# Values matmuls in two halves between the scores, and the last group's end work in small parts

## The chip, the cores and the metric

The kernel runs on one core of a Trainium2 chip. The metric is the device time of one execution in microseconds (us); the time given for a kernel is the median of several runs. In the text TensorE (PE in the profile, PEld its weight loader), VectorE (DVE), ScalarE (ACT), GpSimd (POOL) and SyncE (SP, which here issues the DMAs) are the five engines of the core. They run their own instruction streams in order and meet through semaphores. PSUM has eight banks of 512 32-bit columns by 128 partitions, and TensorE writes only there.

## The reference

One transformer layer, in 32-bit floats, on x of shape (2, 2048, 256):

```python
Q, K, V = (proj(Wq), proj(Wk), proj(Wv))            # 16 heads of 16
# causal attention, online softmax over blocks of 128 keys
scores = scale * einsum('bhtd,bhsd->bhts', Q, kb)
scores = where(future, -inf, scores)
m_new = maximum(m, max(scores)); p = exp(scores - m_new)
l = corr * l + sum(p); acc = corr * acc + einsum('bhts,bhsd->bhtd', p, vb)
O = acc / maximum(l, 1e-12)
x = layernorm(x + O @ Wo.T)
# second part: per-token and per-column absmax scales, round to int8, integer matmul
x = layernorm(x + (q_lhs @ q_rhs) * lhs_scale * rhs_scale)
```

## The kernel before, in words

**Groups and steps.** 32 pairs of batch and head are worked in 8 groups of 4 heads (HG). Within a group the queries are cut into 4 chunks of 512 (CH), and a step (STEPS) is one chunk against one block of 128 keys: 4, 8, 12 and 16 steps for the chunks, 40 (NS) per group. In the last four steps of a chunk the block lies on the diagonal and only 512, 384, 256 or 128 columns of the chunk are worked (skip gives how many are left out).

**A step on TensorE.** For each head j one score: keys by queries, four side-by-side matmuls of 32 output rows (product, line 681), 16-bit parts stacked so that the product is exact enough, into one of 3 PSUM banks (BANKS) that the scores use in turn. ScalarE turns each bank into exponentials in PR (line 974), which frees the bank. After the four scores, values(g, k - 2) follows: for the step two before (LAG = 2), four side-by-side 32-bit matmuls (line 725) of the values and a column of ones on the exponentials into the accumulator bank ps_acc. The profile shows each 32-bit matmul as two records. values waits for the fourth exponential of its step, for GpSimd's mask on the diagonal (line 1289), at a chunk's first step for ScalarE's copy of the accumulator of the chunk before (copy_acc, line 964, semaphore s_accS), and for GpSimd's copy of the values (s_vg). copy_acc stands on ScalarE behind the fourth exponential of a chunk's second step, and waits for the last values of the chunk before.

**Items.** The exponentials need each query's maximum beforehand. So the scores are made a second time, the other way round, one group ahead: an item is two heads of 128 queries by up to 512 keys, in two of four PSUM banks (ps_max, MAX_SLOTS = 2), reduced on VectorE (line 1043). A planner (QUOTA) fixed at build time says after which score how many items have been issued; it works with a fixed cost per score, item and values. The last group has no items.

**End work.** For each chunk of 512 tokens there is an output projection, a residual, a layernorm, the quantised second matmul and the second layernorm, done in two halves of 256 tokens (e, 16 in all). The first six halves run in middle groups through the score banks (soon_parts). The other ten run in the last group and after it, through ps_max: project (two parts, t = 0 and 1; line 796), late "turn" (transposes of the integers, line 818), late "product" (line 796 too). DUE, HALF_START and CHUNK_DUE give at which step each engine puts each part into its stream. The chunks of the second batch are JOINED: the last group's outputs don't go through memory but are taken from accS. For these, token_sums (line 863) turns the sums by token, VectorE inverts them (lines 1189 and 1191), spread_inverses (line 875) spreads them, VectorE multiplies (line 1197), and project adds the last group's part. Each is in order on its engine, so what waits holds back all that is behind it.

**Order of a step in the last group before.** Score 0, score 1, project part 0, score 2, score 3, project part 1, then end_parts (product, turn, token_sums, spread_inverses, finish_projection), then values. After the last group the last two values and the rest of the end work run to the end of the kernel.

## Time and profile before

| | us |
|---|---|
| median of 3 runs | 1014.88 (1013.63 to 1015.7) |
| profiled execution | 1012.61 |
| its span | 1010.9 |
| TensorE, VectorE, ScalarE, GpSimd busy | 950.8, 801.1, 716.4, 271.4 |
| mean granted TensorE clock | 0.988 |

The span runs from the first to the last instruction of the profiled execution; its device time is a little longer. Busy time is the union of an engine's records. TensorE's matmuls overlap in the pipeline, so its records are longer than the distance from one to the next: that distance is to be read from start times. An idle time in brackets is what the engine stood still before the row, with what released it.

### The profile page before, as it was taken

Reading aid. Unit: us, or ns where it says so; the run is one execution under the profiler, and the core shown is the slowest. Engines: PE = TensorE matmul, PEld = TensorE weight load, DVE = VectorE, ACT = ScalarE, POOL = GpSimd, SP = SyncE. Lnnn points to the kernel's source line nnn. Section 1 sums busy time; section 2 is a strip of 40 time slices with the busy share of each in tenths; the row PEclk is TensorE's granted clock in tenths of the full one; section 3 lists DMA queues with packets and bytes.
Section 4 is the critical chain, followed back from the end, with each engine's and each line's share of the span. In section 5 each row is a group of like instructions: output and inputs, shape, how many; then the busy total and the mean of one; then the engine's idle time right before and its main releaser. Section 6 shows DMA issues by size and latency. Waiting matters only on the chain.

```text
span 1010.9 us, 36007 instructions
## 1 busy us (share of the span) xinstructions
PE 950.8 (94%) x15664; PEld 484.8 (48%) x15664; DVE 801.1 (79%) x1081; ACT 716.4 (71%) x1494; POOL 271.4 (27%) x443
## 2 busy tenths in 40 slices
PE   8989999999999999999999999999999999999993
PEld 5645545544544454445444554455545554443432
DVE  4488888887888788878878998999898999566426
ACT  3523458788778877887878877888778877766670
POOL 4433452102210221022213331242214211453322
PEclk9999999999999999999999999999999999999996
DMA  5555440002210221022301240123103204412101
GB/s 176 175 184 160 155 124 13 6 8 55 62 34 9 58 63 29 9 64 66 85 8 48 68 120 10 37 76 90 43 12 91 58 24 120 94 34 75 33 2 42
DMA packets 70846, 66.15 MB, mean 65 GB/s; under 512 B 14704, under 2 KB 65200, under 8 KB 70688
## 3 DMA queue, kind: packets, MB, share of 16 engines
q1 hardware_dynamic: 70688, 63.84, 22.5%
q8 instruction: 124, 2.03, 0.8%
q14 instruction: 34, 0.28, 0.1%
HBM read 42.43 MB, written 20.91 MB: 63 GB/s over the span
## 4 chain that ended last, share of the span: by engine, by line
PE 75%; DVE 13%; ACT 9%; issue 2%; DMA 0%; POOL 0%; POOLq 0%; DVEq 0%; SPq 0%; ACTq 0%
PE ps_acc L725 20%; PE ps_score L681 18%; PE ps_max L681 18%; DVE block_max L1043 9%; ACT PR L974 7%; PE ps_score L604 5%; PE ps_score L611 3%; PE ps_max L796 2%; PE ps_max L679 2%; PE ps_max L699 1%; PE ps_score L796 1%; ACT accS L964 1%; PE ps_acc L585 1%; PE ps_score L710 1%; DVE stats L1143 1%
## 5 line engine op out<-in xcount | busy, mean ns | idle before, releaser
L1043 DVE TENSOR_REDUCE block_max<-ps_max 128x2 f32<-128x1024 f32 (+3 forms) x640 | 653.8, 1060 | 121.0 <-PE ps_max L681 58.0
L974 ACT ACTIVATE PR<-ps_score 128x512 f32<-128x512 f32 (+3 forms) x1280 | 619.8, 542 | 154.7 <-PE ps_score L681 137.2
L681 PE MATMUL ps_score<-QS,KS 99*32 99x512 bf16 (+3 forms) x5120 | 424.1, 350 | 22.2 <-ACT PR L974 18.1
L681 PE MATMUL ps_max<-KS,QS 96*32 96x512 bf16 (+3 forms) x4544 | 328.5, 349 | 7.1 <-DVE block_max L1043 4.7
L725 PE MATMUL ps_acc<-PR,VG 128*32 128x512 f32 (+3 forms) x2560 | 297.2, 530 | 0.0
L681 PEld LDWEIGHTS ps_score<-QS,KS 99*32 99x32 bf16 x5120 | 153.8, 95 | 209.6 <-ACT PR L974 110.2
L681 PEld LDWEIGHTS ps_max<-KS,QS 96*32 96x32 bf16 x4544 | 128.9, 96 | 134.4 <-DVE block_max L1043 62.0
L1289 POOL TENSOR_SCALAR_AFFINE_SELECT PR<-PR 128x512 f32<-128x512 f32 x128 | 81.9, 640 | 281.5 <-ACT PR L974 281.4
L725 PEld LDWEIGHTS ps_acc<-PR,VG 128*32 128x32 f32 x2560 | 82.3, 110 | 29.4 <-issue 0.7
L699 PE MATMUL ps_max<-mask_q,ident_b 128*32 128x64 bf16 (+3 forms) x1808 | 95.7, 200 | 0.0
L1297 POOL CAST max_parts<-neg_max 16x128 bf16<-16x128 f32 (+1 forms) x30 | 9.1, 302 | 201.5 <-ACT neg_max L956 199.0
L604 PE MATMUL ps_score<-PR,wT 128*128 128x512 f32 x128 | 60.4, 597 | 0.8 <-ACT neg_max L934 0.8
L699 PEld LDWEIGHTS ps_max<-mask_q,ident_b 128*32 128x32 bf16 x1808 | 54.9, 97 | 11.1
L916 ACT CAST end_slots<-ps_score 128x512 bf16<-128x512 f32 x32 | 18.7, 585 | 56.7 <-PE ps_score L604 56.7
L1276 POOL TENSOR_TENSOR end_slots<-PR,end_slots 128x512 bf16<-128x512 f32 x32 | 36.9, 1154 | 78.8 <-ACT end_slots L921 78.8
L679 PE MATMUL ps_max<-KS,QS 96*128 96x512 bf16 (+3 forms) x144 | 35.9, 345 | 7.1 <-DVE block_max L1043 7.0
L604 PEld LDWEIGHTS ps_score<-PR,wT 128*128 128x128 f32 x128 | 23.3, 191 | 20.7 <-issue 18.0
L1326 POOL TENSOR_SCALAR var_eps<-moments 128x2 f32<-128x2 f32 x32 | 7.4, 232 | 87.6 <-DVE moments L1149 87.6
L611 PE MATMUL ps_score<-wT,PR 128*128 128x256 f32 x128 | 30.0, 381 | 0.0
L1092 DVE TENSOR_TENSOR PR<-ps_score,end_slots 128x512 f32<-128x512 f32 x32 | 21.7, 683 | 8.0 <-ACT end_slots L916 7.0
L1154 DVE TENSOR_SCALAR end_slots<-end_slots,moments,rstd 128x256 f32<-128x256 f32 x48 | 20.1, 439 | 9.5 <-POOL rstd L1329 9.5
L1281 POOL COPY VG<-V 128x256 f32<-128x256 f32 x32 | 12.7, 396 | 53.4 <-PE ps_acc L725 53.2
(125 smaller groups left out, 556.6 us busy)
## 6 DMA issues: line engine op xcount, KB each, us to landing
QS<-qparts SPq DMA_DIRECT2D x192, 64.0 KB, 2.4
KS<-kparts SPq DMA_DIRECT2D x192, 64.0 KB, 2.4
qparts<-end_slots SPq DMA_DIRECT2D x16, 384.0 KB, 3.7
kparts<-end_slots SPq DMA_DIRECT2D x16, 384.0 KB, 3.1
PR<-in_L_attn_x SPq DMA_DIRECT2D x8, 512.0 KB, 4.5
heads_out<-accS SPq DMA_DIRECT2D x112, 32.0 KB
end_slots<-in_L_attn_x SPq DMA_DIRECT2D x6, 512.0 KB, 7.5
out_y<-end_slots SPq DMA_DIRECT2D x12, 256.0 KB, 2.2
```

Source lines behind the costliest of these rows:

```text
L604: m = pe.matmul(bank, wT[:, w, mh, nh * P:nh * P + P], xT[:, n % 2, mh, :], start=mh == 0, stop=mh == HALVES - 1)
L611: m = pe.matmul(bank[:, t * D:t * D + D], xT[:, n % 2, mh, tile * P:tile * P + P], wT[:, 2, mh, :], start=mh == 0, stop=mh == HALVES - 1)
L679: return pe.matmul(bank[:, 0:w], stack, moving, start=True, stop=stop)
L681: m = pe.matmul(bank[t * QW:t * QW + QW, 0:w], stack[:, t * QW:t * QW + QW], moving, start=True, stop=stop)
L699: m = pe.matmul(bank[r:r + QW, w - P + r:w], ident_b[:, r:r + QW], mask_q[:, r:P], start=False, stop=True)
L725: m = pe.matmul(ps_acc[EYE * j:EYE * j + EYE, s:CH], VG[:, kb, j, :], PR[:, k % 4, j, 0:CH - s], start=kb == 0, stop=k == LAST[c])
L796: y = pe.matmul(out[r:r + QW], stack[:, r:r + QW], moving, start=start, stop=stop)
L974: act.activation(PR[:, k % 4, j, 0:w], ps_score[:, bank_of(use), 0:w], ACT.Exp, scale=SCALE).then_inc(s_exp, 1)
L1043: dve.tensor_reduce(block_max[:, h * PAIR:h * PAIR + PAIR, i, b], ps_max[:, slot_at:slot_at + PAIR, 0:w], AX.X, ALU.max).then_inc(s_reduce ...
L1092: dve.tensor_tensor(rest[:, q % RESTS, :], ps_score[:, u % 3, :], parts[:, n % 2, u, 0, :], ALU.subtract)\
L1276: pool.tensor_tensor(parts[:, n % 2, u, 2, :], rest[:, q % RESTS, :], parts[:, n % 2, u, 1, :], ALU.subtract).then_inc(part3, 1)
L1289: pool.affine_select(out=block, in_=block, compare_op=ALU.is_ge, fill=0.0, base=0, pattern=[[0, HG], [1, P]], channel_multiplier=-1).then_ ...
```

## The change

The values of a step are cut at the middle of their columns. The first half follows the second score (and its items), the second half the fourth; the waits stand in front of the first half, the increment of s_pv behind the second. This holds for all groups; only the last two values after the last group stay whole. In the last group, project is issued in four parts, one behind each score (one half of the contraction each); token_sums, spread_inverses and the turn stand behind the first score, the product behind the third. After the last group the order of the end work is the same as before.

```diff
                             while n < QUOTA[g][k][j]:
                                 on, m = STREAM[KIND[g]][n]
                                 item(*groups[on], m)
                                 n += 1
-                            if j % 2:
-                                project(NS * g + k, j // 2)
-                        end_parts(NS * g + k)
-                        if k >= LAG:
-                            values(g, k - LAG)
-                        elif g:
-                            values(g - 1, NS + k - LAG)
+                            if g == GROUPS - 1:
+                                between_scores(k, j)
+                            elif j % 2 and (g or k >= LAG):
+                                values_half(*divmod(NS * g + k - LAG, NS), j // 2)
...
+                def values_half(g, k, h):
+                    s = skip(*STEPS[k])
+                    middle = s + (CH - s) // 2
+                    if h == 0:
+                        values_wait(g, k)
+                        values_of(k, s, middle)
+                    else:
+                        values_of(k, middle, CH).then_inc(s_pv, 1)
...
+                def values_of(k, a, b):
+                    c, kb = STEPS[k]
+                    s = skip(c, kb)
                     for j in range(HG):
-                        m = pe.matmul(ps_acc[EYE * j:EYE * j + EYE, s:CH], VG[:, kb, j, :], PR[:, k % 4, j, 0:CH - s],
-                                      start=kb == 0, stop=k == LAST[c])
-                    m.then_inc(s_pv, 1)
+                        m = pe.matmul(ps_acc[EYE * j:EYE * j + EYE, a:b], VG[:, kb, j, :], PR[:, k % 4, j, a - s:b - s],
+                                      start=kb == 0 and a == 0, stop=k == LAST[c] and b == CH)
+                    return m
...
+                def between_scores(k, j):
+                    at = NS * (GROUPS - 1) + k
+                    project(at, j // 2, j % 2)
+                    if j == 0:
+                        joins(at)
+                        late_turn(at)
+                    if j == 2:
+                        late_product(at)
+                    if j % 2:
+                        values_half(*divmod(at - LAG, NS), j // 2)
...
-                def project(k, t):
+                def project(k, t, h):
                     for e in late_due(k, f"project{t}"):
                         m, s = divmod(e, 2)
-                        if t == 0:
+                        if t == 0 and h == 0:
                             pe.wait_ge(e_on, HALVES * (m + 1))
...
-                        at = s * HALF + t * P
+                        at, n = s * HALF + t * P, half_rows(m, h)
                         rows = ps_max[:, s, t * D:t * D + D]
-                        for h in range(HALVES):
-                            n = half_rows(m, h)
...
+                        last = h == HALVES - 1
+                        y = tiled(rows, o_in(m)[0:n, h, at:at + P], wT[0:n, 3, h, :], h == 0, last and m not in JOINED)
+                        if last and m in JOINED:
                             y = tiled(rows, accS[:, m % 2, at:at + P], wo_last[:, :], False, True)
```

joins is token_sums and spread_inverses of the step, in that order.

## Rows read from the trace of the kernel before

**Rows 1.** The page, part 1: busy time and share of the span.

```profile
PE 950.8 (94%) x15664; PEld 484.8 (48%) x15664; DVE 801.1 (79%) x1081; ACT 716.4 (71%) x1494; POOL 271.4 (27%) x443
```

**Rows 2.** Stretches: window and length, busy (instructions) by engine, clock, DMA share, GB/s.

```profile
240.90:340.70 99.80, 97.47 (x1868) 48.05 (x1864) 82.29 (x84) 80.43 (x169) 17.23 (x38) 1.00 0.16 40
...
863.20:980.70 117.50, 106.04 (x1587) 45.71 (x1583) 60.82 (x176) 83.01 (x181) 43.67 (x65) 0.97 0.20 51
980.70:1010.90 30.20, 13.49 (x124) 7.73 (x122) 17.01 (x54) 3.04 (x6) 10.12 (x16) 0.70 0.11 35
```

**Rows 3.** Waits of one middle group: who waited for whom, us, times, longest.

```profile
POOL PR L1289 <- ACT PR L974: 37.9, 17, 9.3
...
ACT PR L974 <- PE ps_score L681: 16.4, 42, 1.3
PEld ps_score L681 <- ACT PR L974: 12.1, 37, 0.9
...
PEld ps_max L681 <- DVE block_max L1043: 8.1, 26, 0.5
```

**Rows 4.** TensorE in order of time, a chunk's first steps: start, us, what, xcount.

```profile
341.55 0.61 PE L725 MATMUL ps_acc<-PR,VG 128*32 128x256 f32 x8
341.98 0.34 PE L681 MATMUL ps_score<-QS,KS 99*32 99x384 bf16 x4
...
343.94 0.39 PE L725 MATMUL ps_acc<-PR,VG 128*32 128x128 f32 x8
344.16 0.61 PE L681 MATMUL ps_score<-QS,KS 99*32 99x256 bf16 x12
345.34 0.29 PE L681 MATMUL ps_score<-QS,KS 99*32 99x256 bf16 x4 [0.56 <-ACT PR L974]
345.56 1.06 PE L725 MATMUL ps_acc<-PR,VG 128*32 128x512 f32 x8
346.42 0.27 PE L681 MATMUL ps_score<-QS,KS 99*32 99x128 bf16 x4
```

**Rows 5.** ScalarE in order of time, the same stretch.

```profile
344.41 0.58 ACT L964 COPY accS<-ps_acc 128x512 f32<-128x512 f32 x1
```

**Rows 6.** TensorE in order of time, a plain step of the last group.

```profile
959.63 0.83 PE L681 MATMUL ps_score<-QS,KS 99*32 99x512 bf16 x12
...
960.95 1.03 PE L725 MATMUL ps_acc<-PR,VG 128*32 128x512 f32 x8
961.82 0.82 PE L681 MATMUL ps_score<-QS,KS 99*32 99x512 bf16 x12
```

**Rows 7.** ScalarE in order of time, the same step.

```profile
960.08 2.06 ACT L974 ACTIVATE PR<-ps_score 128x512 f32<-128x512 f32 x4 [1.78 <-PE ps_score L681]
```

**Rows 8.** TensorE in order of time, joins and a projection of the last group.

```profile
878.31 0.40 PE L681 MATMUL ps_score<-QS,KS 99*32 99x512 bf16 x4 [0.58 <-ACT PR L974]
878.64 1.06 PE L863 MATMUL ps_max<-spread,accS 128*128 128x4 f32 x8
879.63 1.52 PE L725 MATMUL ps_acc<-PR,VG 128*32 128x512 f32 x8
...
884.73 0.61 PE L681 MATMUL ps_score<-QS,KS 99*32 99x512 bf16 x8
...
890.02 0.67 PE L681 MATMUL ps_score<-QS,KS 99*32 99x384 bf16 x12
...
911.46 0.64 PE L875 MATMUL ps_max<-ident,last_sums 128*32 128x128 f32 x16 [0.93 <-DVE last_sums L1191]
```

**Rows 9.** Waits of the last group.

```profile
ACT PR L974 <- PE ps_score L681: 32.1, 32, 2.4
...
DVE accS L1197 <- PE ps_max L875: 20.4, 5, 7.3
```

**Rows 10.** VectorE in order of time, last group.

```profile
892.27 0.42 DVE L1197 TENSOR_TENSOR accS<-accS,ps_max 128x256 f32<-128x256 f32 x1 [7.31 <-PE ps_max L875]
```

**Rows 11.** A stretch of the last group, TensorE alone: busy, granted clock.

```profile
880.00:884.00 4.00, 4.00 (x48) 0.57 1.10 219
```

More of the change, by code:

```diff
@@ L811, in end_parts, with late_turn @@
                         y.then_inc(e_prod, 1)
+                def late_turn(k):
                     for e in late_due(k, "turn"):
@@ L820, in end_parts, with joins @@
                         y.then_inc(e_turn, 1)
+                def joins(k):
                     for m in joins_due(k):
@@ L839, in project @@
                                 pe.wait_ge(e_last, LAST_STEPS * joined(m) + 3 + s)
-                        at = s * HALF + t * P
+                        at, n = s * HALF + t * P, half_rows(m, h)
                         rows = ps_max[:, s, t * D:t * D + D]
-                        for h in range(HALVES):
-                            n = half_rows(m, h)
-                            if m == ENDS - 1:
-                                pe.matmul(rows, o_in(m)[0:n, h, at:at + P], wT[0:n, 3, h, :], start=t == 0 and h == 0,
-                                          stop=False)
-                            else:
-                                y = tiled(rows, o_in(m)[0:n, h, at:at + P], wT[0:n, 3, h, :], h == 0,
-                                          h == HALVES - 1 and m not in JOINED)
-                        if m in JOINED and m < ENDS - 1:
+                        if m == ENDS - 1:
+                            pe.matmul(rows, o_in(m)[0:n, h, at:at + P], wT[0:n, 3, h, :], start=t == 0 and h == 0, stop=False)
+                            continue
+                        last = h == HALVES - 1
+                        y = tiled(rows, o_in(m)[0:n, h, at:at + P], wT[0:n, 3, h, :], h == 0, last and m not in JOINED)
+                        if last and m in JOINED:
                             y = tiled(rows, accS[:, m % 2, at:at + P], wo_last[:, :], False, True)
-                        if m < ENDS - 1:
+                        if last:
                             y.then_inc(e_y, 1)
@@ L899, in _ @@
                     for t in range(TPH):
-                        project(k, t)
-                    end_parts(k)
+                        for h in range(HALVES):
+                            project(k, t, h)
+                    late_product(k)
+                    late_turn(k)
+                    joins(k)
+                    for e in due(k, "finish"):
+                        finish_projection(e)
             @block.scalar
```

9 lines of the change are left out of this document (5 added, 4 removed).

## The prediction

> **What bounds the kernel now.** I read the totals first, then stretches, then waits, then the order of time inside single steps. TensorE is busy 950.8 of 1010.9 us, VectorE 801.1, ScalarE 716.4 [rows 1]. TensorE's figure is a union of overlapping records, so 94% is not "full". The stretches show that the eight groups are not alike [rows 2]: a middle group takes 99.8 us with all three engines near 80 to 97; the last group, which has no block-maximum items, takes 117.5 us although ScalarE is busy only 83.0 and VectorE 60.8; 30.2 us of end chain follow the last exponential, with TensorE busy 13.5.
>
> The waits of one middle group go both ways [rows 3]: ScalarE waits 16.4 us for scores while TensorE's weight loader waits 12.1 us for ScalarE to free score banks, and 8.1 us for VectorE. Engines that wait for each other in turn are being fed in lumps that three score banks don't even out; the longest lump is the values. One step's values are 0.86 us (345.56 to 346.42) at 512 columns, 0.43 us (341.55 to 341.98) at 256, 0.22 us (343.94 to 344.16) at 128 [rows 4]. So TensorE sets most of a middle group, but some microseconds of it are waits, and the last group is paced by lumps and by chains. The profiled execution took 1012.61 us (span 1010.9 and 1.7 around it), 2.3 below the median of 1014.88: I work on 1012.6 and add 2.3.
>
> **Values in halves, groups 0 to 6.** The same columns are streamed. Added: each of 318 of the 320 values becomes two halves, and each half is two passes of four side-by-side matmuls (the trace shows eight records a values [rows 4]): 636 sets of four more, each with its weight loads.
>
> Full halves: 2 x 0.43 is 0.86, so a 512-column values in halves costs 0.00 by these rows, 0.02 by their rounding [rows 4]. I take 0.01 x 36 = 0.4 us per group. Four steps of a group have 128 columns, so halves of 64, which the trace doesn't show for this type. Lower end: proportional, 0.11 each, no cost. Upper end: a 64-column half costs as much as the 128-column values, 0.22, so +0.22 a step. The loads are the doubt; I take 0.05 x 4 = 0.2 us per group, 0 to 0.9 being the ends.
>
> The Trainium skill (TensorEngine Tiling (Array Packing), Instruction Overhead) speaks against the change: each matmul carries about 60 cycles of overhead on this chip. At 2.4 GHz that would be an estimate of 25 ns a set and 16 us over 636 sets. By that rule, rows 4 should show half the columns at clearly more than half the time; they don't, so the trace disagrees as long as four run side by side, and the measurement is what my sum uses.
>
> A chunk's start. The first half of values(k-2) now stands behind the second score. For the first step of a chunk it waits for the accumulator copy on ScalarE, which sits behind the fourth exponential of the step before. One such start [rows 4, 5]: the step starts at 344.16 with 256-column scores (0.11 each), so the half would be reached near 344.4; the copy starts at 344.41, takes 0.58 and ends at 344.99. New wait: 0.6 us. Queued behind it on TensorE: scores 2 and 3, the items, so VectorE's food as well. But TensorE waited there already: its fourth score waits 0.56 us for ScalarE [rows 4], and values end at 346.42, 1.43 after the copy. In the new order: half 0.43, score 0.11, score 0.11 (the exponential behind the copy has freed its bank meanwhile), half 0.43: 1.08 after the copy. ScalarE has two scores queued meanwhile. So the wait moves and the step ends 0.35 earlier: 4 x 0.35 = 1.4 us per group. Ends: +0.6 a start (nothing won back) to -0.5.
>
> Elsewhere in a middle group. Of the 12.1 us of waiting for ScalarE, chunk starts hold perhaps 3. Of the other 9 much is hidden behind matmuls in flight (it is the loader's wait). Where four scores come in a row the fourth waits for the first exponential, and half of the values now fills that. I take 0.5 us per group, 0 to 3. Steps with two items and full columns are all TensorE work already and win nothing. The masks of GpSimd are early: it waits 37.9 us in the group for the exponentials that it masks [rows 3], and four more exponentials pass before a half needs the mask. That fails where GpSimd is caught in end work, which I expect once or twice in the last group.
>
> Per group: 1.4 + 0.5 - 0.4 - 0.2 = 1.3 us shorter; over seven groups 9.1. Ends: 1.5 longer to 4 shorter.
>
> **The last group.** Three things move. (a) Plain steps. A step lasts 2.18 us (959.63 to 961.82, of which values run from 960.95, so that four scores took 1.32 where they need 0.88) [rows 6]. ScalarE's four exponentials take 2.06 from first start to last end [rows 7], with the last one's 0.6 overlapping the next start: its own pace is about 1.95 a step. TensorE's content is 4 x 0.22 + 0.86 = 1.74. So the step is set by neither; it is lumps. In halves it should take ScalarE's 1.97: 0.2 shorter. Some 25 of the 40 steps are of this kind or close: 5 us.
>
> (b) Steps with a projection: 884.73 to 890.02 is 5.29 us [rows 8], and TensorE is working through all of it; the pieces are the same. ScalarE starves in it, part of its 32.1 us of waiting for scores in this group [rows 9], but TensorE is the bound: nothing won, only ScalarE kept fed.
>
> (c) Joins, turns and spreads now stand behind the first score, and everything else of the step behind them. Against: the sums by token take 0.99 us (878.64 to 879.63) [rows 8] and now wait for the accumulator copy with one score issued instead of four; the turn of the integers waits for ScalarE's conversion behind the step before; and the spread at 911.46, which waited 0.93 us for VectorE [rows 8], now holds back three scores. If VectorE came no earlier, that alone would cost over 1 us. For: VectorE stood idle 7.31 us until 892.27 for a spread that TensorE issued at the end of its step [rows 10]; that spread now comes a whole step's content sooner, some 3 us, and the chain that ends at 911.46 hangs on it. In all, VectorE waits 20.4 us for spreads in this group [rows 9]. I take the three joins together as 2.5 us won; ends -4 (lost) to +5.
>
> The late mask and narrow halves take 0.5. Sum: 5 + 2.5 - 0.5 = 7.0 us shorter. Ends: 1 to 14; the clock was granted at 0.57 over 880 to 884 [rows 11], part of it at 1.2 GHz, after TensorE had waited 0.58 us for ScalarE at 878.31 and gone through the sums by token, four columns each [rows 8]; fewer waits may give back one or two us, which I leave in the range.
>
> (d) The end chain. Its order after the last step is as before, so 30.2 us stay [rows 2]. SP's and GpSimd's queues keep their order; no DMA is added or moved.
>
> **Sum.** 1012.6 - 9.1 - 7.0 = 996.5; on the median's footing 998.8: I say 999.
>
> **Rivals.**
> 1. Middle groups don't move. The pace there is set by the order of the items and by VectorE (8.1 us of waits for it [rows 3]), and what a half wins is waited away at the next item; costs eat the chunk starts. Only the last group's 7: 1014.9 - 7 = 1008. For: steps with two items have no slack. Against: the waits on ScalarE are the larger.
> 2. The lumps matter more than I count: 3 us a group and 11 in the last (clock given back, VectorE's chain ahead): 1014.9 - 21 - 11 = 983.
> 3. Slower. The half at a chunk's start waits for the accumulator copy and TensorE never recovers it: price 0.45 x 28 starts = 12.6 us, and my 1.4 x 7 = 9.8 credit is void: 999 + 9.8 + 12.6 = 1021. It decides where TensorE reaches the half before the copy ends, while TensorE and not ScalarE is the engine that ends the step. For: the half is reached 0.6 before the copy's end [rows 4, 5]. Against: TensorE already waited 0.56 in that step.
> 4. Each added set has a fixed price that these rows hide, once the halves are short: each half costs as much more as the wait that it fills. Then starts and fills of the middle groups are void, 7 x 1.9 = 13.3, and half of the narrow halves' upper end comes on top, 2.5: 999 + 13.3 + 2.5 = 1015, no change. For: no row shows halves of 64. Against: 0.43 is half of 0.86. The 60 cycles of the Trainium skill's page would come to much the same, its 16 us against my whole gain.
>
> **Chances.** Forecast (990 to 1003) 0.45; rival 1 0.20; rival 2 0.12; rival 3 0.13; rival 4 0.10. A measurement of this kernel tells 0.2%, 2 us, from no change. Faster: 0.45 + 0.20 + 0.12 = 0.77. Same: 0.10. Slower: 0.13. The range that should hold it 8 times in 10 is 985 to 1014: it leaves out most of rival 3 and the far half of rival 2. The likeliest case's own range is 990 to 1003.
>
> **What would show it.** In the profile after: values at 256 columns in sets of 0.43; chunk starts where a values half waits for the accumulator copy and the step is no longer; a middle group near 98.5 us; plain steps of the last group near 1.97 us; the last group near 110 us; VectorE's wait for spreads well under 20 us; end chain still 30 us. Wrong if half sets cost over 0.45 us, if ScalarE waits longer for scores in a middle group than 16.4 us, or if the last group's joins hold TensorE for more than 2 us each.

## The result, and the profile after

| | before | after |
|---|---|---|
| median of 6 runs each | 1014.43 us | 1007.97 us |
| lowest to highest | 1013.56 to 1015.7 | 1005.52 to 1010.32 |
| profiled execution, span | 1012.61, 1010.9 | 1007.38, 1005.7 |
| start of the last group (from the span's start) | 863.2 | 854.4 |
| last group, to the last exponential | 117.5 | 121.5 |
| end chain | 30.2 | 29.8 |

The ratio is 0.9933, 95% interval 0.992 to 0.9946: 6.5 us faster, where 16 were forecast. The two parts of the change went opposite ways. What stands ahead of the last group is 8.8 us shorter (8.3 of it in groups 0 to 6, 0.5 in the stretch before the first group, which the change doesn't touch); the last group is 4.0 us longer.

The page of the kernel after, part 1, answers to [rows 1]:

```profile
PE 944.5 (94%) x18208; PEld 590.9 (59%) x18208; DVE 799.5 (80%) x1081; ACT 719.9 (72%) x1494; POOL 272.0 (27%) x443
```

2544 matmuls and as many weight loads more (318 values with eight more each), 106 us more of loads, and yet less busy time on TensorE. The stretches of the kernel after, columns as in [rows 2]: a middle group, the last group, the end chain.

```profile
239.20:337.90 98.70, 96.34 (x2184) 62.93 (x2180) 82.56 (x84) 80.36 (x168) 17.13 (x37) 1.00 0.15 41
854.40:975.90 121.50, 107.41 (x1909) 55.96 (x1909) 60.16 (x176) 85.77 (x181) 43.99 (x65) 0.94 0.20 49
975.90:1005.70 29.80, 12.68 (x122) 7.67 (x120) 17.01 (x54) 3.01 (x5) 10.11 (x16) 0.66 0.11 36
```

The middle group is 1.1 us shorter (99.8 to 98.7). The last one is 4.0 us longer, at a lower granted clock, 0.94 against 0.97. A last group differs between executions of one order too: the old order took 117.5, 118.0, 119.5 and 120.7 us in the traces of the kernel before and of kernels 11, 1 and 12 below, the new one 121.5 and 120.9 (kernel 2). So the 4.0 of these two traces are not all the change's. The waits of the same middle group, answering to [rows 3]:

```profile
ACT PR L1003 <- PE ps_score L681: 15.5, 41, 0.8
...
PEld ps_max L681 <- DVE block_max L1072: 4.3, 14, 0.5
PEld ps_acc L734 <- ACT PR L1003: 3.3, 4, 0.9
PE ps_acc L734 <- ACT accS L993: 1.9, 4, 0.6
...
PEld ps_score L681 <- ACT PR L1003: 0.9, 4, 0.3
```

Scores no longer wait for a score bank (12.1 us then, 0.9 now) and items wait half as long for VectorE (8.1, now 4.3). The waits that came instead stand at the four chunk starts: TensorE's matmuls wait 1.9 us for the accumulator copy and, at the same places, the weight loader 3.3 us for an exponential. ScalarE is starved nearly as before, 15.5 for 16.4. TensorE in order of time in the kernel after, the chunk start that [rows 4] showed before:

```profile
341.21 0.28 PE L734 MATMUL ps_acc<-PR,VG 128*32 128x64 f32 x8
341.32 0.39 PE L681 MATMUL ps_score<-QS,KS 99*32 99x256 bf16 x8
342.27 0.64 PE L734 MATMUL ps_acc<-PR,VG 128*32 128x256 f32 x8 [0.56 <-ACT accS L993]
342.70 0.43 PE L681 MATMUL ps_score<-QS,KS 99*32 99x256 bf16 x8
342.93 0.64 PE L734 MATMUL ps_acc<-PR,VG 128*32 128x256 f32 x8
343.36 0.27 PE L681 MATMUL ps_score<-QS,KS 99*32 99x128 bf16 x4
```

A half of 64 columns starts at 341.21, the next matmul 0.11 later: half of the 0.22 of 128 columns. A half of 256 takes 0.43 (342.27 to 342.70, 342.93 to 343.36). The first half waits 0.56 us for the copy; from the step's first score to the end of its values it is 2.04 us (341.32 to 343.36), where [rows 4] had 2.26 (344.16 to 346.42). Here the wait moved from the fourth score to the first half, as forecast.

Not every chunk start had a wait to move. TensorE at the start of the third of the four chunks in the group shown (step 14; steps and groups are counted from 0), the fourth score and the values before, and the first half after:

```profile
275.38 0.40 PE L681 MATMUL ps_score<-QS,KS 99*32 99x512 bf16 x4
275.61 1.03 PE L725 MATMUL ps_acc<-PR,VG 128*32 128x512 f32 x8
```

```profile
272.52 0.64 PE L734 MATMUL ps_acc<-PR,VG 128*32 128x256 f32 x8 [0.30 <-ACT accS L993]
```

Before, TensorE stood still at this start for nothing, and neither at step 6; it did for 0.56 and 0.58 us at steps 2 and 26. After, it waits 0.56, 0.49, 0.30 and 0.50 us at steps 2, 6, 14 and 26.

The last group's waits, answering to [rows 9]:

```profile
ACT PR L1003 <- PE ps_score L681: 34.2, 45, 4.9
...
DVE accS L1226 <- PE ps_max L899: 20.3, 5, 6.1
...
PE ps_max L899 <- DVE last_sums L1220: 4.0, 1, 4.0
PE ps_max L887 <- ACT accS L993: 3.5, 3, 1.2
```

The last two lines are what the change brought. VectorE's wait for spreads is as it was, 20.3 us for 20.4. All 4.0 us of the wait for last_sums stand in one place; here it is in order of time, all engines (start, us, engine, line, operation, idle before and releaser):

```profile
894.90 1.03 PE L887 MATMUL ps_max<-spread,accS 128*128 128x4 f32 x8 [1.15 <-ACT accS L993]
...
898.63 0.65 PE L681 MATMUL ps_score<-QS,KS 99*32 99x512 bf16 x4
...
898.96 0.69 DVE L1191 TENSOR_REDUCE amax<-V 128x2 f32<-128x512 f32 x1
...
899.68 1.06 DVE L1197 TENSOR_SCALAR lscale<-amax 128x2 f32<-128x2 f32 x1
...
900.98 1.37 DVE L1206 TENSOR_SCALAR V<-V,linv 128x256 f32<-128x256 f32 x2
902.38 0.43 DVE L1212 TENSOR_SCALAR V<-V 128x512 f32<-128x512 f32 x1
902.72 0.17 DVE L1218 TENSOR_SCALAR last_sums<-ps_max 128x16 f32<-128x16 f32 x1
902.92 0.25 DVE L1220 RECIPROCAL last_sums<-last_sums 128x16 f32<-128x16 f32 x1
903.23 1.08 PE L899 MATMUL ps_max<-ident,last_sums 128*32 128x128 f32 x16 [3.95 <-DVE last_sums L1220]
...
904.09 0.65 PE L681 MATMUL ps_score<-QS,KS 99*32 99x512 bf16 x4
...
904.78 0.60 ACT L1003 ACTIVATE PR<-ps_score 128x512 f32<-128x512 f32 x1 [4.86 <-PE ps_score L681]
```

The granted clock was at half from 42 to 52 us into this group, which is around this wait (see the last section). The sums by token (L887) were done by 896. VectorE inverts them (L1220) only at 902.92: ahead of that in its order stands the rounding of another half (L1191 to L1212). The spread that needs the inverses (L899) now stands behind the FIRST score (898.63), so the second, third and fourth wait with it and ScalarE has nothing for 4.86 us. Before, the same spread stood behind all four scores and waited 0.93 us [rows 8]; in three more executions of that order (kernels 1, 11 and 12 below) it waited nothing, nothing and 1.98 us. In kernel 2, with the new order, it waited 2.89.

A plain stretch of the last group after, one whole step and the start of the next, to set against [rows 6]:

```profile
954.62 0.62 PE L681 MATMUL ps_score<-QS,KS 99*32 99x512 bf16 x8
955.05 0.62 PE L734 MATMUL ps_acc<-PR,VG 128*32 128x256 f32 x8
955.49 0.62 PE L681 MATMUL ps_score<-QS,KS 99*32 99x512 bf16 x8
955.94 0.61 PE L734 MATMUL ps_acc<-PR,VG 128*32 128x256 f32 x8
956.38 0.71 PE L681 MATMUL ps_score<-QS,KS 99*32 99x512 bf16 x8
```

### The profile page after: what moved, and what is told of

Same layout as the page of the kernel before. It is cut to its first block, busy times and chain, and to the rows that moved or that the text cites. A ratio compares the mean times of both kernels' runs of the same rounds, so it can differ in the third digit from the quotient of the medians.

```text
span 1005.7 us, 41095 instructions
## 1 busy us (share of the span) xinstructions
PE 944.5 (94%) x18208; PEld 590.9 (59%) x18208; DVE 799.5 (80%) x1081; ACT 719.9 (72%) x1494; POOL 272.0 (27%) x443
## 4 chain that ended last, share of the span: by engine, by line
PE 77%; DVE 10%; ACT 6%; SPq 3%; issue 2%; POOL 1%; DMA 1%; POOLq 0%; ACTq 0%; DVEq 0%
PE ps_acc L734 20%; PE ps_score L681 19%; PE ps_max L681 18%; DVE block_max L1072 6%; PE ps_score L604 5%; ACT PR L1003 4%; PE ps_score L611 3%; PE ps_max L824 2%; PE ps_max L679 2%; SPq L439 2%; PE ps_max L699 2%; PE ps_score L824 1%; ACT accS L993 1%; PE ps_acc L585 1%; DVE end_slots L1183 1%
## 5 line engine op out<-in xcount | busy, mean ns | idle before, releaser
L1003 ACT ACTIVATE PR<-ps_score 128x512 f32<-128x512 f32 (+3 forms) x1280 | 627.2, 539 | 160.4 <-PE ps_score L681 141.7
L681 PE MATMUL ps_score<-QS,KS 99*32 99x512 bf16 (+3 forms) x5120 | 452.3, 350 | 3.3 <-ACT PR L1003 2.2
L734 PE MATMUL ps_acc<-PR,VG 128*32 128x256 f32 (+1 forms) x5104 | 367.7, 350 | 10.5 <-ACT accS L993 9.1
L681 PE MATMUL ps_max<-KS,QS 96*32 96x512 bf16 (+3 forms) x4544 | 335.1, 348 | 5.5 <-DVE block_max L1072 2.9
L681 PEld LDWEIGHTS ps_score<-QS,KS 99*32 99x32 bf16 x5120 | 169.4, 96 | 96.5 <-ACT PR L1003 22.5
L734 PEld LDWEIGHTS ps_acc<-PR,VG 128*32 128x32 f32 x5104 | 170.2, 110 | 83.7 <-ACT PR L1003 16.2
L681 PEld LDWEIGHTS ps_max<-KS,QS 96*32 96x32 bf16 x4544 | 138.5, 96 | 88.4 <-DVE block_max L1072 37.7
L699 PE MATMUL ps_max<-mask_q,ident_b 128*32 128x96 bf16 (+3 forms) x1808 | 99.1, 200 | 0.0
L1172 DVE BATCH_NORM_STATS2 stats<-end_slots 128x6 f32<-128x256 f32 x48 | 19.0, 417 | 12.0 <-POOL end_slots L1374 11.8
L679 PEld LDWEIGHTS ps_max<-KS,QS 96*128 96x128 bf16 x144 | 13.3, 97 | 24.3 <-DVE block_max L1072 13.1
```

The lines of the kernel that those rows point to most:

```text
L679: return pe.matmul(bank[:, 0:w], stack, moving, start=True, stop=stop)
L681: m = pe.matmul(bank[t * QW:t * QW + QW, 0:w], stack[:, t * QW:t * QW + QW], moving, start=True, stop=stop)
L699: m = pe.matmul(bank[r:r + QW, w - P + r:w], ident_b[:, r:r + QW], mask_q[:, r:P], start=False, stop=True)
L734: m = pe.matmul(ps_acc[EYE * j:EYE * j + EYE, a:b], VG[:, kb, j, :], PR[:, k % 4, j, a - s:b - s], start=kb == 0 and a == 0, stop=k == LAS ...
L1003: act.activation(PR[:, k % 4, j, 0:w], ps_score[:, bank_of(use), 0:w], ACT.Exp, scale=SCALE).then_inc(s_exp, 1)
```

## The experiments

All were timed in five rounds beside the kernel before. Times are medians; ratios are to the kernel before in the same rounds, and kernels of different rounds are compared by ratio. Step times below are from ScalarE's first exponential of a step to that of the next. Medians of kernels whose ratios differ by less than 0.002 to 0.003 (2 to 3 us) can't be told apart.

**1. Halves in groups 0 to 6 alone** (e1_middle_only) and **2. the last group's change alone** (e2_last_only).

```diff
# 1, against after: between_scores, the last group
-                    project(at, j // 2, j % 2)
-                    if j == 0:
-                        joins(at)
-                        late_turn(at)
-                    if j == 2:
-                        late_product(at)
-                    if j % 2:
-                        values_half(*divmod(at - LAG, NS), j // 2)
+                    if j % 2:
+                        for h in range(HALVES):
+                            project(at, j // 2, h)
+                    if j == HG - 1:
+                        late_product(at)
+                        late_turn(at)
+                        joins(at)
+                        values(*divmod(at - LAG, NS))
# 2, against after: groups 0 to 6
-                            elif j % 2 and (g or k >= LAG):
-                                values_half(*divmod(NS * g + k - LAG, NS), j // 2)
+                            elif j == HG - 1 and (g or k >= LAG):
+                                values(*divmod(NS * g + k - LAG, NS))
```

> Values in halves in groups 0 to 6; the last group as before, values whole, end work after the fourth score. Theory A (the middle groups won what was forecast, the last group lost because joins, turns and spreads wait behind the first score with three scores behind them): 8 to 9.5 us faster than before, about 1005.5; the last group at 117 us as before, its step 15 at about 4.8. Theory B (middle groups and last group can't be told apart, the gain of the one is lost in the other whatever is done): about 1008, with the last group longer than 117.5.

> Values whole behind the fourth score in groups 0 to 6 (as before); the last group as in the changed kernel. Theory A: 3 to 5 us slower than before, about 1018, the last group 121 us, one spread wait of 4 us. Theory B: within 1 us of before.

Measured: 1005.1, ratio 0.9899 (0.9884 to 0.9913); and 1016.86, ratio 1.0024 (1.0014 to 1.0035). The halves of the middle groups are worth 10 us; the last group's part as a whole costs 2.4 alone, and 3.4 on top of the other (0.9933 less 0.9899). So the forecast's 9.1 for the middle was right in size, its 7.0 for the last group had the wrong sign. Theory A holds for both times by and large, though 2.4 us is less than its 3 to 5. In the traces kernel 1's last group is not at 117 as expected but at 119.5 us, with step 15 at 3.37 us and step 14 at 5.84, where the kernel before has 4.81 and 3.97: single steps shift between executions of one order. Steps 13 to 16 together do so less: 17.0, 17.4, 17.5 and 18.6 us with the old order (before, kernels 1, 11, 12), 21.2 and 22.0 with the new one (after, kernel 2).

**3. Which of the pieces costs: turn and joins back behind the fourth score** (e3_joins_last); **4. only the spread back** (e4_spread_last).

```diff
# 3
-                    if j == 0:
-                        joins(at)
-                        late_turn(at)
+                    if j == HG - 1:
+                        late_turn(at)
+                        joins(at)
# 4: the loop of joins() that calls spread_inverses is now spreads()
+                    if j == HG - 1:
+                        spreads(at)
```

> The changed kernel, with turn, sums by token and spread of a step in the last group behind the fourth score (before the second half of the values) instead of behind the first; projection and product still in small parts. Theory A: the last group falls from 121 to 110 to 113 us (the plain steps' 5 us are won), 8 to 11 us faster than the changed kernel: about 998. Rival C (the small parts of the projection between the scores are what delays the masks and with them the chain over GpSimd and VectorE, not the place of the joins): the last group stays at 118 us or more, about 1005.

> The changed kernel, with the spread alone behind the fourth score; sums by token and turn stay behind the first. Theory A with the spread's wait at step 15 as the one large loss: 3 to 5 us faster than the changed kernel, about 1004, steps with sums by token still 1 us long in waiting. Rival C: no more than 1 us faster.

Measured: 1003.28, ratio 0.9887 (0.9874 to 0.99); and 1007.46, ratio 0.9929 (0.9911 to 0.9946). The third gives back 4.7 us, so those places cost; but its last group is 118.4 us, where rival C had it, far from theory A's 110 to 113. The fourth gives back nothing that can be told (0.4 us, give or take 2). TensorE's spread of the second join in the third and in the fourth kernel, in order of time:

```profile
902.74 1.08 PE L899 MATMUL ps_max<-ident,last_sums 128*32 128x128 f32 x16 [3.09 <-DVE last_sums L1220]
```

```profile
903.67 0.77 PE L902 MATMUL ps_max<-ident,last_sums 128*32 128x128 f32 x16 [2.03 <-DVE last_sums L1224]
```

With the spread three scores later the waits are 3.09 and 2.03 us, against 3.95 and 2.89 in the two executions with it behind the first score. The inversion that ends them comes 48.6 to 49.6 us into the group in all of kernels 1 to 4 and the kernel after: TensorE's order doesn't set that point, VectorE's own does. In kernel 4 the spreads of the other joins moved too, and by steps that costs: steps 10, 18, 28 and 30, which hold a projection, take 5.06 or 5.07 us where they took 4.33, 4.88, 4.76 and 4.77, and step 9 takes 0.45 less. That is about 1 us back out of the 1.9 that steps 13 to 16 are shorter (19.3 for 21.2), and what is left is too small for the medians.

**5. The kernel after, with VectorE's inversion one step earlier** (f1_after_invert_early); **6. the same edit on kernel 3** (f2_joins_last_invert_early); **7. halves in all groups with all end work whole and at its old places** (f3_halves_all_endwork_old); **8. the early inversion in the kernel before** (f4_before_invert_early).

```diff
# 5, 6, 8 (VectorE): the second join's inversion one step earlier
-                    for m in joins_due(k):
-                        invert_last(m)
+                    for m in JOINED:
+                        if HALF_START[2 * m] - (2 if m == JOINED[0] + 1 else 1) == k:
+                            invert_last(m)
# 7, against kernel 1
-                        values(*divmod(at - LAG, NS))
+                    if j % 2:
+                        values_half(*divmod(at - LAG, NS), j // 2)
```

> The changed kernel, with one edit on VectorE: the inversion of the second join's sums (chunk 5) stands one step earlier in VectorE's stream, ahead of the first layernorm and rounding of half 9 instead of behind them; no work added or left out. Theory D (the last group is held by VectorE's chain: the inversion comes 48 to 50 us after the group's start in all five kernels so far, 6 us after its sums were ready, and the spread behind it holds back TensorE, now with three scores behind it): inversion at 42 to 43 us, the 4 us wait at step 15 gone, 4 to 6 us faster than the changed kernel, about 1003. Rival C (the placing of the parts between the scores is itself what costs, the wait would only move to the next part): within 1.5 us of the changed kernel's 1008.

> The same edit on VectorE, on the kernel in which turn, sums by token and spread stand behind the fourth score (1003.3). Theory D: steps 15 and 16 fall from 14.1 us together to about 10, 3 to 5 us faster than 1003.3: about 999. Rival C: within 1.5 us of 1003.

> Values in halves in all groups, the last one too, but the last group's end work whole and at its old places (project behind the second and fourth score, the rest behind the fourth). Tells the small parts from the halves in the last group. If the small parts themselves cost (rival C): faster than the kernel with joins behind the fourth score and small parts (1003.3), about 1001. If only the joins' place and VectorE's chain matter: 1003 to 1004, and against the kernel with old last group (1005.1) 1 to 2 us faster for the plain steps.

> The kernel before with the same edit on VectorE alone. Theory D: there the spread waited only 0.93 us, so 1 to 2 us faster than before, about 1013; the inversion at about 43.5 us after the group's start. Rival C: no difference.

Measured:

| kernel | median | ratio (interval) | last group | steps 13 to 16 |
|---|---|---|---|---|
| before | 1014.43 | 1 | 117.5 | 17.0 |
| after | 1007.97 | 0.9933 (0.992 to 0.9946) | 121.5 | 21.2 |
| 5 after, early inversion | 1001.73 | 0.9872 (0.9854 to 0.9891) | 116.2 | 17.3 |
| 6 kernel 3, early inversion | 1004.18 | 0.9886 (0.9867 to 0.9905) | 120.2 | 20.7 |
| 7 halves, old end work | 1000.42 | 0.9863 (0.984 to 0.9886) | 115.7 | 18.5 |
| 8 before, early inversion | 1016.16 | 1.0004 (0.9993 to 1.0015) | 122.2 | 18.8 |

Kernel 5 is one edit on VectorE, with TensorE's order untouched, and it wins 6 us, as theory D said. The inversion in its trace, VectorE in order of time, and then the same twelve microseconds (44 to 56 into the last group) in the kernel after and in kernel 5, columns as in [rows 2]:

```profile
896.39 0.17 DVE L1218 TENSOR_SCALAR last_sums<-ps_max 128x16 f32<-128x16 f32 x1
896.60 0.25 DVE L1220 RECIPROCAL last_sums<-last_sums 128x16 f32<-128x16 f32 x1
```

```profile
898.40:910.40 12.00, 7.91 (x116) 3.87 (x108) 6.52 (x15) 4.77 (x9) 4.71 (x5) 0.65 0.18 64
```

```profile
897.80:909.80 12.00, 11.87 (x200) 5.97 (x196) 6.85 (x17) 8.04 (x16) 4.76 (x5) 0.85 0.28 79
```

The inversion comes at 42.8 us instead of 48.6, TensorE is busy 11.87 of 12 us instead of 7.91, and ScalarE 8.04 instead of 4.77. Step 15 falls from 8.88 us to 3.60 while step 14 grows from 3.70 to 5.08; steps 13 to 16 together fall from 21.2 to 17.3, to what the old order took. In kernel 5 no wait of TensorE for the inverses is left. So the cause of the larger loss is shown: TensorE waited for a late producer on VectorE. How much of its price comes from the three scores behind the wait is not shown as well: kernel 4 took them out from behind it, and steps 13 to 16 were 1.9 us shorter. The rest of kernel 5's 6 us goes with shorter half-clock stretches (10.2 us of the group for 13.7), which one trace each can't settle.

Kernel 6 did what rival C said: no gain, steps 15 and 16 at 14.2 us where theory D had 10. Its trace says why. TensorE, in order of time:

```profile
908.13 1.08 PE L824 MATMUL ps_max<-wT,V 128*32 128x256 f32 x8 [3.59 <-DVE accS L1226]
```

And VectorE:

```profile
907.23 0.43 DVE L1212 TENSOR_SCALAR V<-V 128x512 f32<-128x512 f32 x1
907.57 0.42 DVE L1226 TENSOR_TENSOR accS<-accS,ps_max 128x256 f32<-128x256 f32 x1
```

With the inverses early, the projection of the next step (wT is its operand; behind the first score) waits 3.59 us for VectorE's multiplication by the spread inverses (L1226). That one stands in VectorE's order behind the same layernorm and rounding of half 9 (from 901.56 to the end of L1212), which before had stood ahead of the inversion. So the wait changed its place, but not its cause. (The profiled execution, 1008.66 us, is the slowest of its five; 3 us of that stand in group 3, as told below under the middle groups.) Kernel 7 keeps the late inversion, and its spread, behind four scores, still waits:

```profile
903.05 1.08 PE L900 MATMUL ps_max<-ident,last_sums 128*32 128x128 f32 x16 [2.83 <-DVE last_sums L1221]
```

Yet it has the lowest median of all, though kernels 3, 5, 6, 9 and 10 can't be told from it: 7.1 us better than after by the ratios, and 3.7 better than kernel 1, which differs from it only in the last group's values being whole (the two intervals just touch, so it may be 1 or 6). Those 3.7 are what halves alone bring there; I had forecast 5. By steps: steps 17 to 39 take 62.2 us in each of the four traces of the old order without other edits and 59.0 in kernel 7, 3.2 less; with the new order they take 60.9 (kernels 2 and 5; 62.5 in the kernel after, where a half-clock stretch lies in steps 26 and 27).

Kernel 8 is as the kernel before, which rival C said and theory D (1013) did not; its inversion comes at 46.6 us and not at 43.5.

**9. Kernel 7 with the early inversion** (g1_endwork_old_invert_early); **10. kernel 7 with only the projection in small parts** (g2_projection_small_only).

```diff
# 10, against 7
-                    if j % 2:
-                        for h in range(HALVES):
-                            project(at, j // 2, h)
+                    project(at, j // 2, j % 2)
```

> Halves of the values in all groups, the last group's end work whole and at its old places, and on VectorE the inversion of the second join (join chunk 5) one step earlier. Without the early inversion this kernel measured 1000.4 us; there the second join's spread waited 2.83 us for VectorE and step 15 of the last group took 6.72 us. Theory D (the second join waits for VectorE, and the wait is paid by TensorE wherever the spread stands): the 2.8 us go, 997 to 998.5, step 15 at 4.5 us or less. Rival E (only a spread behind the FIRST score is dear, since it holds three scores back; behind the fourth, ScalarE's queue of scores hides most of it): within 1 us of 1000.4, with the group's length unchanged but for half-clock stretches, as in the kernel before, where the same edit did nothing.

> Halves in all groups; of the last group's end work only the projection is in small parts (one behind each score); product, turn, sums by token and spread stand whole behind the fourth score, as before the change. The kernel with projection and product between scores and the rest behind the fourth measured 1003.3 us; with all of it at the old places 1000.4. Theory P (small parts of the projection are what costs: they put 4 more switches between scores, and ScalarE gets its scores late): about 1003, last group 118. Rival Q (the product behind the third score is what costs, since the turn that feeds it is now late and the product waits with a score behind it; small parts of the projection are even or win): 1000 or below, last group 115 to 116.

Measured: 1003.01, ratio 0.9881 (0.9863 to 0.9898), last group 114.8; and 1002.48, ratio 0.9879 (0.9856 to 0.9902), last group 116.4. Neither can be told from kernel 7 (0.984 to 0.9886). The ninth is not at theory D's 997 to 998.5, and its step 15 takes 5.63 us and not 4.5; rival E (within 1 us of 1000.4) is nearer, but not by its mechanism: the 2.83 us of the spread went, and the projection's wait for the multiplication came, as in kernel 6. That one, and the row that sums it with the first join's projection, 22 us into the group (0.99 us; it stands ahead of the edit, and the kernel after has it too, with 0.73):

```profile
904.93 1.21 PE L825 MATMUL ps_max<-wT,V 128*32 128x256 f32 x16 [1.78 <-DVE accS L1227]
```

```profile
PE ps_max L825 <- DVE accS L1227: 2.8, 2, 1.8
```

The same happened in kernel 8:

```profile
916.31 1.21 PE L796 MATMUL ps_max<-wT,V 128*32 128x256 f32 x16 [1.13 <-DVE accS L1197]
```

But TensorE doesn't wait in every order. The tenth kernel has the late inversion (48.9 us), and its spread hardly waits, since TensorE comes to it later:

```profile
907.30 0.65 PE L898 MATMUL ps_max<-ident,last_sums 128*32 128x128 f32 x16 [0.17 <-DVE last_sums L1219]
```

The late inversion comes at 47.9 to 49.6 us in all ten kernels that have it; the wait is what TensorE has left when it gets there, 0 to 2 us in the old last group, 2.9 to 3.95 in the new one.

The tenth's median, 1002.48, lies near theory P's 1003 and can't be told from 1000.4; its last group (116.4) lies between P's 118 and rival Q's 115 to 116. By steps the small parts do cost: against kernel 7 steps 18, 28 and 30, which hold a projection, take 5.06 us for 4.86 each, and the last step 2.99 for 2.29; all steps but 13 to 16 together are 1.7 us longer. So theory P is borne out in part. Against kernel 3, which has the product behind the third score, the ratios (0.9879, 0.9887) can't be told apart, so rival Q's price of the product isn't shown.

**11. Both halves side by side behind the fourth score, groups 0 to 6** (e5_halves_adjacent); **12. halves in groups 0 to 6 but for the chunk starts** (e6_starts_whole). Both with the last group as before.

```diff
# 11, against kernel 1
-                            elif j % 2 and (g or k >= LAG):
-                                values_half(*divmod(NS * g + k - LAG, NS), j // 2)
+                            elif j == HG - 1 and (g or k >= LAG):
+                                for h in range(2):
+                                    values_half(*divmod(NS * g + k - LAG, NS), h)
# 12, against kernel 1, in values_half
+                    if STEPS[k][1] == 0:
+                        if h:
+                            values(g, k)
+                        return
```

> Groups 0 to 6: the values are issued as two halves, but both side by side behind the fourth score, so that only the number of matmul sets differs from the kernel before (two sets where there was one); the last group is as before. My forecast's terms (0.4 + 0.2 us a group for the sets): 4.2 us slower than before, 1018 to 1019. Rival (a set more costs nothing that can be measured, as rows with half the columns in half the time say): 1014 to 1015, groups within 0.3 us of those before. The Trainium skill's 60 cycles a matmul (TensorEngine Tiling (Array Packing), Instruction Overhead) would make it some 14 us over 560 sets: 1028.

> Groups 0 to 6 in halves, last group as before, but the values at a chunk's start (4 a group, 28 in all) whole and behind the fourth score as before. With those in halves too it measured 1005.1, before the change 1014.4: 9.3 us won in groups 0 to 6. My forecast put 9.8 us of gain in these 28 steps (0.35 each) and 3.5 less 4.2 in all the others: then about 1014. Rival S (the gain is spread over all full steps, and the starts are like the others, 28 of 280 steps): 1006 to 1007. Rival T (the half at a start, which waits for the accumulator copy, costs: it is better whole): 1003 to 1004.

Measured: 1015.18, ratio 1.0001 (0.9989 to 1.0012); and 1009.43, ratio 0.9945 (0.9924 to 0.9965). The second middle group of kernels 11, 12 and 1, columns as in [rows 2]:

```profile
241.20:341.20 100.00, 97.67 (x2185) 58.06 (x2181) 82.30 (x84) 80.45 (x169) 17.24 (x38) 1.00 0.16 41
```

```profile
240.80:339.70 98.90, 97.08 (x2152) 62.15 (x2148) 82.36 (x84) 79.98 (x168) 17.14 (x37) 1.00 0.16 41
```

```profile
239.50:338.20 98.70, 96.35 (x2188) 62.72 (x2184) 82.57 (x84) 80.34 (x169) 17.13 (x37) 1.00 0.16 41
```

The sets themselves cost 0.2 us a group (100.0 against 99.8), under what a median can tell; my forecast's 4.2 us for them (1018 to 1019) is not there, the rival's 1014 to 1015 is. The gain is all in the place between the scores. In the group shown the chunk starts hold 0.2 us of the 1.1 (98.9 against 98.7), the other steps 0.9, the sets' own cost taken off. The four starts are not alike: halves at the start win 0.24 us in step 2 and 0.2 in steps 26 and 27, win nothing at step 6 and lose 0.26 in step 14. The ratios give the starts more: 0.9945 less 0.9899 is 4.6 us of 10, by the two intervals anything from 2 to 7. In the profiled execution of kernel 12, the slowest of its six, groups 3 to 6 are 3.8 us longer than in kernel 1, of which 0.6, 0.7 and 0.9 come in single steps (14 and 22 of group 3, 23 of group 5) that differ between executions of one order. So what the starts are worth can't be settled closer. All of it is under the 9.8 that I had given them: neither that forecast (1014) nor rival S (1006 to 1007) nor rival T (1003 to 1004) is where kernel 12 came out.

## Why the prediction was right and wrong

**Middle groups: right in sum by luck, wrong in make-up.** Forecast 1.3 us a group and 9.1 in all; measured 1.1 in the group shown, 8.3 in groups 0 to 6 by the trace, and 10 (ratio 0.9899) with kernel 1. Inside it, chunk starts were to bring 1.4 a group and brought 0.2 in the group shown (0.65 if the ratios are taken as they stand), the fills elsewhere 0.5 and brought about 1.1, and the added sets were to cost 0.6 and cost 0.2. Three errors cancelled. I had discounted most of the 12.1 us of [rows 3], the loader's wait for score banks, as hidden behind matmuls. That was right: the wait fell to 0.9, VectorE's halved beside it, and with 15 us less of these waits, against 5 us of new ones, the group got 1.1 us shorter. The ends that I gave the sum don't follow from its terms either: these give 3.7 us longer to 4.6 shorter, not 1.5 to 4.

**Chunk starts.** The mechanism was right for the start that I had read: 0.56 us of wait where 0.6 was forecast, and no wait at the fourth score; the step ended 0.22 earlier, not 0.35. The error was to take one start for four. "TensorE waited there already" held at two of them in the group shown (0.56 and 0.58 us) and not at steps 6 and 14, where the wait for the copy (0.49 and 0.30) is new. Rival 3 (TensorE never recovers) is refuted, and rival 1 (middle groups don't move).

**A wait that the change brought in group 3.** In the kernel before, and in kernels 2 and 8, whose groups 0 to 6 are the same, group 3 takes 103.9 us each time. In the ten kernels with halves between the scores in groups 0 to 6 it takes from 101.3 to 106.1, and most of the spread stands in step 14. VectorE and TensorE in kernel 10:

```profile
471.13 0.20 DVE L1156 TENSOR_SCALAR sums<-sums 128x64 f32<-128x64 f32 x1 [2.42 <-DMA sums<-row_sums]
```

```profile
472.78 1.04 PE L681 MATMUL ps_max<-KS,QS 96*32 96x512 bf16 x8 [2.85 <-DVE block_max L1071]
```

VectorE stands still for a DMA of row sums, the block maxima stand behind it, and TensorE's next item waits for them. The DMA wait is 0 to 2.46 us in those ten traces, TensorE's wait 0.33 to 2.88; the three kernels with whole values have neither there. I had not looked at this step. It is part of why medians of kernels with the same middle groups scatter by some us, and it has nothing to do with the last group; what makes the DMA late in some executions stays open.

**Halves cost nothing.** 0.43 and 0.11 us, as the columns say. The Trainium skill's 60 cycles a matmul (TensorEngine Tiling (Array Packing), Instruction Overhead) would have made kernel 11 some 14 us slower, an estimate, if they came on top of each matmul's columns; the ratio 1.0001 disagrees with that where four matmuls run side by side. The page's own example says less: a matmul of one column takes as long as one of 60. Taken so, it says nothing against halves of 64 and more, and no run here tests it. Rival 4 is refuted: 80 more sets in a group cost 0.2 us.

**Plain steps, (a).** Steps 19, 31 and 32 of the last group (counted from 0), of the kind of [rows 6], fell from 2.18 to 1.92 us; I had said 1.97. The plain stretch above shows it: four scores and a whole values from 954.62 to 956.38, 1.76 us of content with no gap left. But few of the 25 steps that I counted are of this kind, and some got longer in halves alone (kernel 7 against before): step 4 by 0.85 us, step 23 by 0.48, step 39 by 0.37. The whole is 3.7 us (kernel 7 against kernel 1) or 3.2 (steps 17 to 39); the medians alone don't tell that from 5.

**Joins, turn and spread, (c): the step that failed.** I took the three joins as 2.5 us won, with 4 lost as an end. The kernel after is 7.1 us slower than kernel 7, which has the old places. I wrote "that spread now comes a whole step's content sooner, some 3 us, and the chain that ends at 911.46 hangs on it". That is true only of the first join: VectorE got its spread at 882.35, 28.0 us into the group, where it had been 29.1. In all, VectorE waited for spreads as long as before (20.3 us), where "well under 20" was to show the gain, and my sign of being wrong, joins that hold TensorE for more than 2 us, came true at 3.95. The second join's spread depends on an inversion that VectorE's own order puts behind another half's rounding. It came at 48.6 us (47.9 before). TensorE arriving earlier at that wait bought nothing, and three scores stood behind it. I had written the danger down ("if VectorE came no earlier, that alone would cost over 1 us") and priced it by the 0.93 us of [rows 8], the wait as seen from the old place in one execution. Seen from the new one it is 3.95 (2.89 in kernel 2), and steps 13 to 16 take 21.2 and 22.0 us where the old order took 17.0 to 18.6: about 4 us lost where 2.5 were to be won. The rest of the loss is smaller: the sums by token wait 1.15 us three times for the accumulator copy, behind one score, where they had waited for nothing; the small parts of the projection cost something (kernel 10); and the four steps whose turn now stands behind the first score with no other end work around it (22, 24, 34, 36) took 11.6 us in all where they had 9.8, of which the steps right after 22 and 36 give back part.

Last group, by steps from ScalarE's exponentials, after less before: steps 13 to 16 +4.2, steps 22, 24, 34 and 36 +1.7, step 26 +1.4 (it lay in a half-clock stretch, so this is not the order's; the same step in kernel 2, with the same order in this group, took 3.38 and not 4.78), all others together -3.3. The sum is +4.0.

**End chain.** 29.8 for 30.2: as forecast.

**The rivals.** The time landed on rival 1's 1008 by chance, not by its mechanism: the middle groups moved in full, and the last group took back nearly half of it. Rival 2 (983) needed 3 us a group; there were 1.1.

**What stays open.** Which of kernels 3, 5, 6, 7, 9 and 10 is best: their ratios, 0.9863 to 0.9888, can't be told apart. What the three scores behind the wait cost by themselves: kernel 4 answers it only within about 2 us. How much of the difference between two last groups is half clock and how much is order. What an order of VectorE would bring in which both the inversion and the multiplication stand ahead of half 9's rounding: with the early inversion alone the wait came back at the projection in kernels 6, 9 and 8 (3.59, 1.78 and 1.13 us), and only in kernel 5 did TensorE come late enough to wait for neither.

## What to carry to other kernels

Here cutting a lump of TensorE work in two cost next to nothing (0.2 us for 80 more sets of four side-by-side matmuls), and setting the halves between the feeds of another engine paid 1.1 us a group. That is a tenth of what the loader had waited for banks: such a wait, which stands behind matmuls in flight, is not a gain to count on. One chunk start, read closely, was not four: read each place that a term is multiplied by. Before an instruction is moved forward in one engine's queue, read when its producer is done in absolute time, and price the wait from the new place with everything that then stands behind it: the wait shown at the old place (0.93 us here, and 0 to 2 us in other executions of the same order) is not its price. Where the producer is late by its own engine's order, one edit there can win back the loss (6 us in kernel 5), but in kernels 6, 8 and 9 the same edit was worth nothing, since the next link of the same chain, the multiplication, still stood behind the same rounding.

## What was not expected of the hardware

The last group of one and the same order differs by microseconds between executions, by where stretches of half clock fall. The kernel after, TensorE alone, a stretch 83 us into the last group, and then all engines in the same stretch of kernel 2, whose order there is the same:

```profile
937.60:941.10 3.50, 3.50 (x48) 0.52 0.00 0
```

```profile
947.20:950.70 3.50, 3.50 (x68) 2.48 (x72) 2.28 (x9) 2.40 (x6) 1.05 (x3) 1.00 0.02 5
```

48 matmuls at 1.2 GHz against 68 at 2.4 GHz in 3.5 us. Kernel 2 had such stretches 17 and 41 us into the group (17.1 us in all), the kernel after at 42 and 83 (13.7 us), the kernel before at 17 and 44 (6.8 us). The old last group took 117.5 to 120.7 us in four executions, with 6.8 to 13.7 us at half clock. So a difference of up to 3 us between last groups of two single traces isn't a finding by itself. Most of its steps that no half-clock stretch touches repeat to some hundredths of a us between executions of one order. The experiments above are read by these, by single waits and by medians.
